# Second scan on one Trainium2 core: units of images j and j+4, spread in 32-row tiles of the array

## The reference, cut to what matters

```python
xz = xf @ W_in                       # xf: pixels x 8 tokens x 8 channels
xs = concatenate([xp, xp[:, ::-1]])  # both directions over the 8 tokens
dts, Bs, Cs = split(xs @ W_x)
delta = softplus(dts @ W_dt + 2 * b_dt)
# scan over 8 tokens, state 16 wide for each of 16 inner channels:
h = exp(delta * A) * h + (delta * u)[:, :, None] * B[:, None, :]
y = einsum('bdn,bn->bd', h, C)
```

## Time and profile before

| | us |
|---|---|
| median of 3 runs | 2016.04 (2014.6 to 2017.21) |
| profiled execution, its own time | 2014.68 |
| its span, first to last instruction | 2012.7 |
| PE busy / weight loads | 1651.0 / 979.8 |
| DVE busy | 1585.5 |
| ACT busy | 1158.2 |
| POOL busy | 1168.7 |
| mean granted TensorE clock (1 is 2.4 GHz) | 0.942 |

### The profile page before, as it was taken

How to read it: one execution, slowest core, us unless ns; L and a number is a source line. 1 busy time by engine, 2 the same in 40 slices (tenths; PEclk the granted TensorE clock), 3 DMA queues, 4 the chain that set the end, 5 groups by cost and what they waited for, 6 DMA issues and landing times. The chain is left out here.

```text
span 2012.7 us, 31048 instructions
## 1 busy us (share of the span) xinstructions
PE 1651.0 (82%) x9878; PEld 979.8 (49%) x9878; DVE 1585.5 (79%) x1549; ACT 1158.2 (58%) x1889; POOL 1168.7 (58%) x881
## 2 busy tenths in 40 slices
PE   5888787996788888888888888657888888888787
PEld 2555444884444454444545544234555554554333
DVE  3788745554799999999999999441899999999854
ACT  3444484334666666666666665265666665665356
POOL 0666501001467767676776775202899999999701
PEclk8999988997899999999999999777999999999898
DMA  4000000000254444444444444200000000000001
GB/s 135 2 0 0 1 0 1 1 1 1 53 95 88 90 90 87 94 83 94 89 89 83 94 91 92 44 1 0 1 1 0 0 0 0 0 0 0 7 5 42
DMA packets 23435, 78.21 MB, mean 39 GB/s; under 512 B 3792, under 2 KB 4816, under 8 KB 23120
## 3 DMA queue, kind: packets, MB, share of 16 engines
q0 software_dynamic: 18432, 67.12, 17.6%
q1 hardware_dynamic: 4944, 10.35, 1.8%
HBM read 8.25 MB, written 2.10 MB: 5 GB/s over the span
## 5 line engine op out<-in xcount | busy, mean ns | idle before, releaser
L1173 POOL TENSOR_TENSOR s_prod<-s_ahead,s_cs 128x1024 f32<-128x1024 f32 x128 | 312.2, 2439 | 203.7 <-DVE s_back L1150 103.1
L1708 POOL TENSOR_TENSOR r_prod<-r_state,r_cs 128x512 f32<-128x512 f32 x256 | 322.4, 1298 | 14.8 <-DVE r_state L1649 14.2
L1147 DVE TENSOR_TENSOR_SCAN s_ahead<-s_fore,s_pfeed 128x1024 f32<-128x1024 f32 x128 | 292.7, 2287 | 11.8 <-ACT s_fore L1069 5.3
L1150 DVE TENSOR_TENSOR_SCAN s_back<-s_aft,s_pfeed 128x1024 f32<-128x1024 f32 x128 | 289.5, 2261 | 0.0
L1069 ACT ACTIVATE s_fore<-s_pd,s_aneg 128x896 f32<-128x896 f32 x128 | 129.7, 1013 | 161.0 <-PE s_pd L940 161.0
L940 PE MATMUL s_pu<-s_partsu,selr 128*128 128x512 f32 x512 | 173.4, 462 | 52.2 <-DVE s_pfeed L1140 52.0
L1636 DVE TENSOR_TENSOR r_feed<-r_pu,r_bs 128x512 f32<-128x512 f32 x256 | 164.4, 687 | 61.9 <-PE r_pu L1478 61.9
L1140 DVE TENSOR_TENSOR s_pfeed<-s_pu,s_bs 128x1024 f32<-128x1024 f32 x128 | 157.8, 1233 | 37.7 <-PE s_pu L940 25.0
L1601 ACT ACTIVATE r_decay<-r_pd,r_aneg 128x512 f32<-128x512 f32 x256 | 168.3, 686 | 23.2 <-PE r_pd L1478 23.0
L1478 PE MATMUL r_pu<-r_parts,selr 128*128 128x512 f32 x512 | 161.3, 437 | 5.7 <-DVE r_feed L1636 5.7
L1649 DVE TENSOR_TENSOR_SCAN r_state<-r_decay,r_carry,r_feed 128x512 f32<-128x512 f32 x128 | 156.3, 1263 | 0.0
(11 more groups left out here) (255 smaller groups left out, 3338.1 us busy)
## 6 DMA issues: line engine op xcount, KB each, us to landing
s_ahead<-s_back POOLq DMA_DIRECT2D x128, 512.0 KB, 4.5
x_act<-in_x_dram SPq DMA_DIRECT2D x8, 256.0 KB, 5.4
out_dram<-x_act SPq DMA_DIRECT2D x16, 128.0 KB, 2.3
k_scan<-in_pack_scan_dram SPq DMA_DIRECT2D x1, 1600.0 KB, 10.4
k_fir<-in_pack_fir_dram SPq DMA_DIRECT2D x1, 1600.0 KB, 13.8
k_l<-in_pack_l_dram SPq DMA_DIRECT2D x1, 450.0 KB, 6.9
k_ln<-in_pack_ln_dram SPq DMA_DIRECT2D x3, 131.0 KB, 3.0
k_mlp<-in_pack_mlp_dram SPq DMA_DIRECT2D x2, 194.0 KB, 5.1
```

Of the source, the lines that this page charges most:

```text
L1147: dve.tensor_tensor_scan(ahead[:, v % 4], f, feed[:], 0.0, ALU.mult, ALU.add).then_inc(ahead_done, 1)
L1150: dve.tensor_tensor_scan(back[:, v % 4, ::-1], a[:, ::-1], feed[:, ::-1], 0.0, ALU.mult, ALU.add).then_inc(back_done, 1)
L1173: pool.tensor_tensor(prod[:, b], ahead[:, v % 4], cs[:, buf].rearrange("p i n -> p (i n)"), ALU.mult).then_inc(prod_done, 1)
L1708: pool.tensor_tensor(prod[:, v % 2, q], state[:, v % 2, q], cs[:, v % UNROLL // 4, q], ALU.mult).then_inc(multiplied, 1)
```

## The change

It lies in the program of PE and in `place`, which PE and ACT use. No instruction is added to or taken from any engine.

- A unit has images j and j+4 in place of 2j and 2j+1, and the pairs come in the order j = 0, 2, 1, 3.
- A spread takes only the 32 rows in which its selector is not zero, as a 32-row tile of the array (`tile_position=(image // 2 * 32, 0)`). The two images of a unit are 64 rows apart, so in two different tiles, and write into two different banks.
- For u and d the four matmuls of a unit are issued as high part of the first image, high part of the second, low part of the first, low part of the second. For B and C one image is spread at a time, as before.
- An output matmul writes two runs of 64 columns in place of one of 128.

```diff
         def place(u):
             u %= UNROLL2
-            return u // 8, u % 8 // 2, u % 2
+            return u // 8, (0, 2, 1, 3)[u % 8 // 2], u % 2
...
-            def spread(bank, sel, parts):
+            def spread(banks, sels, images, parts):
                 for part in range(2):
-                    mm = pe.matmul(bank, selr[:, sel * P:(sel + 1) * P], parts[:, part], start=(part == 0),
-                                   stop=(part == 1))
+                    for bank, sel, image in zip(banks, sels, images):
+                        rows = slice(image // 2 * 32, image // 2 * 32 + 32)
+                        mm = pe.matmul(bank, selr[rows, sel * P:(sel + 1) * P], parts[rows, part], start=(part == 0),
+                                       stop=(part == 1), tile_position=(image // 2 * 32, 0))
                 return mm
...
-                    for i in range(2):
-                        mm = spread(ps_u[:, i * N:(i + 1) * N], 2 * (2 * j + i) + g, parts_u[:, half])
-                    mm.then_inc(u_rep, 1)
+                    spread((ps_u[:, 0:N], ps_u[:, N:2 * N]), (2 * j + g, 2 * j + 8 + g), (j, j + 4),
+                           parts_u[:, half]).then_inc(u_rep, 1)
...
-                    for i in range(2):
-                        mm = spread(ps_d[:, i * N:(i + 1) * N], 2 * (2 * j + i) + g, parts_d[:, half])
-                    mm.then_inc(d_ps, 1)
+                    spread((ps_d[:, 0:N], ps_d[:, N:2 * N]), (2 * j + g, 2 * j + 8 + g), (j, j + 4),
+                           parts_d[:, half]).then_inc(d_ps, 1)
...
-                    spread(ps_m[:], 16 + 2 * j + i, (parts_b, parts_c)[second][:, half]).then_inc(
+                    spread((ps_m[:],), (16 + j + 4 * i,), (j + 4 * i,), (parts_b, parts_c)[second][:, half]).then_inc(
                         (b_rep, c_rep)[second], 1)
...
-                            mm = pe.matmul(ps_y[quad * 32:(quad + 1) * 32, j * NPX:(j + 1) * NPX],
+                            mm = pe.matmul(ps_y[quad * 32:(quad + 1) * 32].rearrange(
+                                               "p (b h n) -> p h b n", h=HALVES, n=PX)[:, j % 2, j // 2::2],
```

## The result

| | before | after |
|---|---|---|
| median, us | 2015.86 | 2105.49 (2099.53 to 2110.93, 4 runs) |
| ratio | | 1.0447, 95% interval 1.0424 to 1.047 |
| span of the profiled execution | 2012.7 | 2097.6 |
| DVE busy | 1585.5 | 1585.2 |
| mean granted TensorE clock | 0.942 | 0.795 |

The change makes the kernel 4.5% slower, 90 us, all of it in the second scan: s_pfeed, VectorE's first instruction of a unit, starts for the first time at 507.7 us (509.0 before) and for the last time at 1343.3 (1258.9 before). The instructions are as many as before, and VectorE's take as long (1585.2 us in all, 1585.5 before).

What follows compares the result with a forecast made beforehand. VectorE was taken to bound the second scan at 5.84 us a unit. Saving 3.5 us at its start and 1.1 us of later waits gave 4.6 us, so 2011.4 us against the median, range 2007.5 to 2019.

Steps and rivals of the forecast that it cites:

- The sum: Second scan: 3.5 us saved at its start and 1.1 us of later waits for ScalarE's decay, 4.6 us in all.
- part (3): Spreads of B and C: one image in one tile, nothing runs side by side, so the effect is 0.
- the clock rival: Start of the second scan: more TensorE waiting lowers its clock and cancels the saving, 2014 to 2017 us; chance 22%.
- What bounds the kernel now: Second scan: VectorE's own time, 5.84 us a unit, untouched by the change; only the excess over it can go.
- The overlap (1): Spreads of u and d run two at a time, saving 0.93 us a unit, 1.6 to 1.7 at the low clock.
- The switches (2): Changes between full-height and 32-row matmuls cost 0.3 us each, 0.5 at the low clock; eight per eight units.
- The first unit: Start of the second scan: half the spread slots save 1.57 us; first forward scan s_ahead at 509.74 instead of 511.31.
- (a): Sign of overlap: four s_pd matmuls, the spreads of d, take about 0.6 to 0.75 us instead of 1.08.
- (c): Sign at s_pu, the spreads of u, behind a full matmul: its first load waits for that matmul's end.
- (d): Sign in the second scan: the period of s_ahead is 5.84 us from the seventh unit on; above that, VectorE no longer bounds.
- (e): Sign: VectorE's waits for s_fore and s_pu after the first total below 3 us, against 7.1 before.
- (f): Sign: TensorE's granted clock between 510 and 545 us; below 0.8 the clock rival holds.

Runs made afterwards that it cites:

- e1: The changed kernel with every spread taking all 128 rows again, pairs and striped output kept: 2015.94 us, ratio 1.0002 to the kernel before.
- e6: The changed kernel with u and d in pairs of 64-row tiles and B and C at 128 rows: 2013.27 us, ratio 0.9992 to the kernel before.
- e3: The changed kernel with 32-row tiles for u and d only, B and C at 128 rows: 2025.32 us, ratio 1.0054 to the kernel before.
- e4: The changed kernel with u and d at 128 rows and only B and C in 32-row tiles: 2045.06 us, ratio 1.0154 to the kernel before.
- e7: The kernel before with only its spreads put in 32-row tiles, both images of a unit in the same rows: 2280.38 us, ratio 1.1311.
- e2: The changed kernel with the first image's high and low parts issued ahead of the second's: 2109.69 us, ratio 1.0469 to the kernel before.

## Why the prediction was wrong

The step that failed is the clock. The sum took TensorE's lengths from the trace of before and let the clock fall in the first 30 us at most; part (3) gave the 32-row spreads of B and C the price 0, and the clock rival closed with "Later a low clock is covered". The runs showed a granted clock of 0.62 in the middle of the stage where it had been 0.98, held down by the height of the tiles, and 86.1 us more between the scans.

- *What bounds the kernel now*: right, for the clock of before. VectorE's instructions kept their length, and where the clock held (e1, e6) the period stayed at 5.84.
- *The overlap (1)*: right in mechanism, somewhat oversized: 0.35 to 0.41 us of saving per four matmuls at the high clock (0.66 to 0.73 against 1.07), 0.46 forecast. At the low clock 2.08 to 1.22, 0.86, near the 0.8 forecast.
- *The switches (2)*: 0.37 us of loader idle at the high clock (e3), 0.65 and 0.44 at the low one (into and out of the negative identity at 1013.51 and 1014.23), for my 0.3 and 0.5. Right in kind. The count of eight in a group is short: the program also changes shape ahead of each full matmul and ahead of the skip matmuls. What those cost isn't separated.
- *Part (3), "0; they get the same two records"*: this is a step that failed. The records are the same, their rows are not. Taking three quarters of the height from B and C, where nothing overlaps, costs 1.5% with the switches that it brings (e4), and with u and d at 32 rows it is the difference between 2025 (e3) and 2105, though e3 has more switches.
- *The clock rival*: named, with a row for it, and priced at nothing. Two errors. I tied the fall to waiting alone; for this fall e7, 93% busy at 0.53, refutes that. And I let it act in the first 30 us only, with "Later a low clock is covered, as in 882 to 888". A single window of low clock is covered; a lasting one is not. My own figure for a cycle at the low clock, 7.7 us, was there, and it held where no negative identity lies in the cycle (7.63, 7.58 at the start); with it the cycle is 8.6 to 8.8, since its two switches come on top. Carried over the stage, (7.7 - 5.84) x 4 x 16 groups would have been 119 us, and not nothing. That it comes near the measured 86 is two errors against each other: fewer units are stretched (38, not 64), and each by more (2.4 us, not 1.9).
- *The first unit*: 3.23 us from s_pu to s_ahead, 2.9 forecast. The first s_ahead at 509.58 seems to meet the forecast 509.74, by luck: s_pu itself started 0.44 us earlier than before.
- *The signs named*: (a) came true, 0.66 us for four s_pd at the high clock (e3). (c) came true, the first load of s_pu at 1012.36 for a full matmul that ends at 1012.43. (d) and (e) failed: distances of 8.83 in the middle of the stage, and 97.7 us of waits where below 3 were expected. (f) named the cause: the clock of 510 to 545 is 0.50, below 0.8. The rival's low clock was there; its reason (waiting) and its time (2014 to 2017) were wrong.

## What to carry to other kernels

A matmul cut to the rows that matter can lose more in TensorE's clock than it wins in time: before tiling, look at what else the engine does, and keep the spreads that don't overlap at full height, or take the tallest tile that still separates the operands (64 rows here). Even that won nothing clear of the noise in this kernel (e6, 0.9992), since the overlap shortens the work of an engine for which VectorE hardly waited. When a rival changes a clock, price it over the whole stage and not only over the stretch in which the trace already shows it.

## What the runs showed that was not expected

- The clock of the stage's middle follows the height of the spreads (u and d / B and C): 128/128 0.99, 64/128 0.97, 128/32 0.93, 64/64 0.88, 32/128 0.84, 32/32 0.62, and 0.53 for 32/32 without overlap.
- Matmuls in different row tiles overlap in either order of the program: two start together at 903.74 and two at 904.34 in e2, though each image's high and low parts are issued one behind the other.
- The 16 output matmuls in column tiles take 1.14 us at the low clock and 1.11 at the high one, while the full matmuls of 512 columns nearly double (1.10 and 2.04): the clock hardly changes the pace of the former.
